# Attention and a conditional convolution on one core: turns of four key tiles, eight probability buffers, streamed experts

## The chip, the cores and the metric

The kernel runs on one core of one Trainium2 chip. The metric is the time of one execution on the device in microseconds (us), the median of the runs shown.

## The reference, cut to what matters

Sixteen images of 256 channels and 32 x 32 pixels (N = 1024 positions) go through two layers, all in float32.

```python
# layer 0: attention, 4 heads of 64
xn = group_norm(x, gn_w, gn_b)                       # 32 groups
q, k, v = split(qkv_w @ xn + qkv_b)
p = softmax(q^T k / 8)                               # 1024 x 1024 per head
x = x + proj_w @ (v p^T) + proj_b
# layer 1: conditional bottleneck, 8 experts
rw = sigmoid(mean(x) @ router_w^T + router_b)        # per image
w1, w2, w3 = sum_e rw[e] * experts[e]                # 1x1, 3x3, 1x1
h = relu(bn1(conv1x1(x, w1))); h = relu(bn2(conv3x3(h, w2)))
out = relu(bn3(conv1x1(h, w3)) + x)
```

## The kernel before

**Stages.** The program is a prologue, one section per image (`sections`: images 0, 1 and 15 written out, 2 to 14 a loop) and an epilogue. A section does the attention of its image i; the projection, the router and the convolutions of image i-1 and the normalisation, Q, K and V of image i+1 are "side jobs" in it. Every engine walks the same tables in the same order, so a table fixes the order of each engine's instructions, and semaphores do the rest.

**Attention.** A section has 4 blocks (2 head pairs x 2 halves of 512 queries) of 8 key tiles, so 32 steps. A step s on TensorE is `scores` (L574 and L577, two float32r matmuls for each of two heads, into one of two S slots; `scores(s)` waits for the exponential of step s-2), then ScalarE's exponential over 1,024 columns (L654) into one of PBUF probability buffers, GpSimd's running sum of the probabilities (L447, `psum_p`), and `pv` (L590, true float32, two heads in the two 64-column halves of the array). `z` (L492) sums `psum_p` over the keys with ones. The scores have the row maximum subtracted inside the matmul: for every step TensorE also fills MS with Q K^T of a later block (`max_fill`, L555, AHEAD = 4 + 8 steps ahead), VectorE takes the maximum (L763), `row` (L503, L767) turns eight of them into a row, and two DMAs of SyncE (L336) carry it into Q2, where the second scores matmul (L577) of the block's first step waits for it. MS is one buffer, so fill n+1 waits for maximum n:

```python
pe.wait_ge(max_read, 32 * i + 8 * b + m)
```

**Turns.** A turn is two steps: scores(2t+2), fill, MID jobs; scores(2t+3), fill, LATE jobs; pv(2t), pv(2t+1); HALVES jobs. The jobs all use one PSUM bank, SB. Each carries `held`, the job before it, and waits on TensorE until that one has been read out of SB:

```python
for k, bi, bf in before:
    pe.wait_ge(read[k], done(k, bi, bf))
```

**Who reads the jobs.** ScalarE reads `qk` (L668 to a raw copy, L672 twice to the float32r part), `v` (L678, L679), `z` (L683), `conv1` (L694, relu into `hpad`) and `conv2` (L698). VectorE reads `proj` (L805; after the fourth also `pool2` L810 and `poolb` L813, which `router` L514 waits for), `router` (L816), `conv3` (L825, then relu L702 and a store L361 into one of 3 y slots), `gna`, `gnb` and `row`. VectorE further does `split_x` (L755), the low parts of Q and K (L800), the gates (L841, L843), the weighted sum of experts (`mix_experts`, L851 and L854, 8 per image), the copies into `mix3` (L859), `stats` (L749) and `normalise_o` (L836). The exact places on VectorE are: maximum, jobs of the half step, then the extras of the tables MIX, RECIPROCAL, NORMALISE, SPLIT, STATS.

**DMA.** SyncE issues everything in the order of the tables: the copies `dup` of Q and K to the other partition half, `rows`, the round trip of z for the reciprocals (`move_z`, `spread_z`: rz to zc, reciprocal L831 on 64 x 16, z_dram, back as rz), `shift_h` (hpad's lower half to the upper one shifted by one, before conv2), the stores and the loads of x, V and, once, all 8 experts (`ex`, 24 KB per partition).

Of the kernel before, what the change touches and what calls it, by code (L numbers as in the profile page):

```python
# [36 lines left out]
P = 128  # L37
# [21 lines left out]
PBUF = 4  # L59
# [10 lines left out]
TURNS = STEPS // 2  # L70
# [10 lines left out]
EPILOGUE = ([("z", 0, 3)] + [("proj", 0, f) for f in range(4)] + [("router", 0, 0), ("conv1", 0, 0),  # L81
# [15 lines left out]
def build(nc, x, vecs, router_b, wqkv, wproj, wrouter, experts, neg_eye, group_avg, out):  # L97
    ctx = ExitStack()
    with ctx:
# [16 lines left out]
        ex = sb("ex", [P, E, MIX])  # L116
# [13 lines left out]
        x_lo = sb("x_lo", [P, CC, N], F32R)  # L130
        Q1 = sb("Q1", [P, HEADS, N], F32R)
# [5 lines left out]
        prob = sb("prob", [P, PBUF, 2, HALF])  # L137

# [48 lines left out]
        xin_loaded = sem("xin_loaded")  # L187
        x2_loaded = sem("x2_loaded")
# [16 lines left out]
        h_saved = sem("h_saved")  # L205
# [62 lines left out]
        def jobs_of(place, t, first, last):  # L268
            return [j for j in place.get(t, []) if not (first and j[1] < 0) and not (last and j[1] > 0)]

        def all_jobs(t, first, last):
            return jobs_of(MID, t, first, last) + jobs_of(LATE, t, first, last) + jobs_of(HALVES, t, first, last)
# [29 lines left out]
        def _(sp):  # L302
# [36 lines left out]
            def shift_h(i):  # L339

                sp.wait_ge(read["conv1"], i + 1)
                sp.dma_start(hpad[64:128, 0:PAD], hpad[0:64, 1:PAD + 1]).then_inc(h_saved, 16)

# [13 lines left out]

            def store(i, f):
                oc, hf = f // NH, f % NH
                sp.wait_ge(y_ready, 4 * i + f + 1)  # L360
                sp.dma_start(out[i, :, oc, px(hf)], y[:, f % YBUF, :]).then_inc(y_stored[f], 16)  # L361

            def section(i, first, last):
                load_v1(i)
                if not last:
                    load_xin(i + 1)
                for t in range(TURNS):
                    for kind, di, f in all_jobs(t, first, last):
# [4 lines left out]
                        if kind == "conv1":  # L373
                            shift_h(i + di)
                        if kind == "conv3":
                            store(i + di, f)
                        if kind == "z":
                            move_z(i + di, f)
                    if t in RECIPROCAL and in_range(RECIPROCAL[t][0], first, last):
                        spread_z(i + RECIPROCAL[t][0], RECIPROCAL[t][1])  # L380
                load_x2(i)
# [9 lines left out]
            sp.dma_start(ex[:, :, :], experts).then_inc(rest_loaded, 16)  # L391
# [5 lines left out]
            move_z(B - 1, BLOCKS - 1)  # L397
            spread_z(B - 1, BLOCKS - 1)
            shift_h(B - 1)
# [55 lines left out]
        def _(pe):  # L455
# [9 lines left out]
            def job(kind, i, f, before, bank=SB[:, :], at_end=False):  # L465
# [38 lines left out]
                elif kind == "bias":  # L504

                    pe.wait_ge(rest_loaded, 16 * 5)
# [14 lines left out]
                elif kind in ("conv2a", "conv2"):  # L521
                    if kind == "conv2a":
                        pe.wait_ge(h_saved, 16 * i + 16)
# [90 lines left out]
            def section(i, first, last):  # L614

                kind, di, f = all_jobs(TURNS - 1, isinstance(i, int) and i == 1, False)[-1]
                held = [("row", 0, 0)] if first else [(kind, i - 1 + di, f)]
                for t in range(TURNS):
                    for half, place in ((0, MID), (1, LATE)):
                        if t < TURNS - 1:  # L620
                            scores(i, 2 * t + 2 + half)
                        elif not last:
                            scores(i + 1, half)
                        at = fill_at(i, 2 * t + half, last)
                        if at:
                            max_fill(*at)
                        for kind, di, f in jobs_of(place, t, first, last):
                            job(kind, i + di, f, held)
                            held = [(kind, i + di, f)]
                    pv(i, 2 * t)  # L630
                    pv(i, 2 * t + 1)
                    for kind, di, f in jobs_of(HALVES, t, first, last):
                        job(kind, i + di, f, [] if kind == "conv2" else held)
                        held = [(kind, i + di, f)]

            sections(pe, section)
            pe.wait_ge(read["z"], BLOCKS * B - 1)
# [6 lines left out]
        def _(act):  # L644
# [16 lines left out]
            def job(kind, i, f, bank=SB[:, :]):  # L661
# [25 lines left out]
                elif kind == "conv1":  # L687
                    act.wait_ge(filled["conv1"], i + 1)
                    rows_hf = H // NH
                    for hf in range(NH):  # L690
                        at = (1 + hf * rows_hf) * PW + 1
                        dst = hpad[0:64, at:at + rows_hf * PW].rearrange("p (r w) -> p r w", w=PW)[:, :, 0:W]
# [30 lines left out]
            def section(i, first, last):  # L723
                for t in range(TURNS):
                    for half, place in ((0, MID), (1, LATE)):
                        if t < TURNS - 1:
                            exps(i, 2 * t + 2 + half)
                        elif not last:
                            exps(i + 1, half)
                        for kind, di, f in jobs_of(place, t, first, last):  # L730
                            job(kind, i + di, f)
                        if t == NORM and not last:
                            normalise(i + 1, half)
                    if t % 4 == 3:
                        save_o(i, t // 4)
                    for kind, di, f in jobs_of(HALVES, t, first, last):
                        job(kind, i + di, f)
# [7 lines left out]
        def _(dve):  # L745
# [82 lines left out]
            def reciprocal(i, f):  # L828

                dve.wait_ge(z_moved[f], 32 * i + 32)  # L830
                nc.vector.reciprocal(zc[:, f % 2, :], zc[:, f % 2, :]).then_inc(rz_ready, 1)  # L831

            def normalise_o(i, f):
                dve.wait_ge(z_back[f], 32 * i + 32)
# [11 lines left out]
            def mix_experts(i, e0, e1):  # L846
                for e in range(e0, e1):
                    if e == 0:
                        gates(i)
                        wait(dve, filled["conv3"], 4 * i)  # L850
                        nc.vector.tensor_scalar(mix[:, :], ex[:, 0, :], rw[:, 0:1], None, ALU.mult).then_inc(mix_chain, 1)  # L851
                    else:
                        dve.wait_ge(mix_chain, E * i + e)
                        nc.vector.scalar_tensor_tensor(out=mix[:, :], in0=ex[:, e, :], scalar=rw[:, e:e + 1], in1=mix[:, :],  # L854
# [7 lines left out]
            def mix_last(i):  # L862

                gates(i)
                n = E * i
                for c0, c1 in ((0, M1), (M1, M1 + M2), (M1 + M2, MIX)):
                    for e in range(E):
                        if e == 0:
                            if c0 == 0:
                                dve.wait_ge(filled["conv3"], 4 * i)  # L870
                            op = nc.vector.tensor_scalar(mix[:, c0:c1], ex[:, 0, c0:c1], rw[:, 0:1], None, ALU.mult)
                        else:
                            dve.wait_ge(mix_chain, n)
                            op = nc.vector.scalar_tensor_tensor(out=mix[:, c0:c1], in0=ex[:, e, c0:c1], scalar=rw[:, e:e + 1],
# [42 lines left out]
            dve.wait_ge(rest_loaded, 16 * 5)  # L917

            def section(i, first, last):
                mixed = 0  # L920
                for t in range(TURNS):
                    for half, place in ((0, MID), (1, LATE)):
                        at = fill_at(i, 2 * t + half, last)
                        if at:
                            max_reduce(*at)
                        for kind, di, f in jobs_of(place, t, first, last):
                            job(kind, i + di, f)
                        if half == 1 and t in RECIPROCAL and in_range(RECIPROCAL[t][0], first, last):
                            reciprocal(i + RECIPROCAL[t][0], RECIPROCAL[t][1])
                        if half == 1 and t in NORMALISE and in_range(NORMALISE[t][0], first, last):  # L930
                            normalise_o(i + NORMALISE[t][0], NORMALISE[t][1])
                        if not last:
                            if half == 1 and t == STATS_0:
                                stats(i + 1, 0)
                            if half == 1 and t == STATS_1:
                                stats(i + 1, 1)
                            if t == SPLIT:
                                split_x(i + 1, half)
# [72 lines left out]
```

## Time and profile before

| | |
|---|---|
| median of 3 runs (lowest to highest) | 2105.53 us (2100.91 to 2111.38) |
| profiled execution, its own time | 2096.82 us |
| its span | 2095.0 us |
| mean granted TensorE clock | 0.984 |
| busy: TensorE, VectorE, GpSimd, ScalarE | 94%, 69%, 53%, 50% |
| chain that ended last | PE 79%, DVE 12%, issue 5%, DMA 2%, ACT 2% |
| HBM | 34 GB/s over the span |

The first `conv1` matmul of an image is at 254.1, 380.5, 506.4, 632.2, 759.6 us and so on to 1900.0: one image takes 125.8 to 127.4 us. The epilogue begins at about 2044. Busy TensorE is an upper bound of its work, since the ends of matmuls are modelled; the distances between starts are what counts. In the rows further down, a timeline row has the start and the duration in us, the number of merged instructions (x8) and in brackets the idle time ahead of it with what ended it.

### The profile page before, as it was taken

Reading aid. Unit: us, or ns where it says so; the run is one execution under the profiler, and the core shown is the slowest. Engines: PE = TensorE matmul, PEld = TensorE weight load, DVE = VectorE, ACT = ScalarE, POOL = GpSimd, SP = SyncE. Lnnn points to the kernel's source line nnn. Section 1 sums busy time; section 2 is a strip of 40 time slices with the busy share of each in tenths; the row PEclk is TensorE's granted clock in tenths of the full one; section 3 lists DMA queues with packets and bytes.
Section 4 is the critical chain, followed back from the end, with each engine's and each line's share of the span. In section 5 each row is a group of like instructions: output and inputs, shape, how many; then the busy total and the mean of one; then the engine's idle time right before and its main releaser. Section 6 shows DMA issues by size and latency. Waiting matters only on the chain.

```text
span 2095.0 us, 26308 instructions
## 1 busy us (share of the span) xinstructions
PE 1960.1 (94%) x8072; PEld 1061.8 (51%) x8072; DVE 1440.0 (69%) x1638; ACT 1045.7 (50%) x1346; POOL 1118.7 (53%) x533
## 2 busy tenths in 40 slices
PE   4999999999999999999999989999899999999994
PEld 3555555545555455555555545455554555545431
DVE  5658768486784957758586785857858587685743
ACT  3555545454555444555454555454554455554441
POOL 3665555464555545555464564645555555554660
PEclk9999999999999999999999999999999999999997
DMA  3112131121313012130121312113130121301201
GB/s 137 42 26 82 36 101 26 44 74 31 101 31 96 20 36 91 32 105 20 41 81 31 101 30 65 47 36 96 31 101 18 38 87 34 101 24 43 56 27 61
DMA packets 65694, 119.35 MB, mean 57 GB/s; under 512 B 20480, under 2 KB 21248, under 8 KB 65536
## 3 DMA queue, kind: packets, MB, share of 16 engines
q1 hardware_dynamic: 65664, 118.97, 19.4%
q8 instruction: 16, 0.26, 0.1%
q14 instruction: 14, 0.11, 0.0%
HBM read 54.68 MB, written 17.04 MB: 34 GB/s over the span
## 4 chain that ended last, share of the span: by engine, by line
PE 79%; DVE 12%; issue 5%; DMA 2%; ACT 2%; DVEq 0%; SPq 0%; POOL 0%; ACTq 0%
PE PV L590 19%; PE SB L461 12%; PE S L574 11%; PE MS L555 10%; PE S L577 9%; PE SB L498 5%; PE SB L532 4%; DVE mx L763 4%; DVE mix L854 3%; PE SB L492 3%; PE SB L540 3%; DVE rden L841 2%; PE SB L519 1%; DVE o L836 1%; DVE x_lo L755 1%
## 5 line engine op out<-in xcount | busy, mean ns | idle before, releaser
L447 POOL TENSOR_TENSOR psum_p<-psum_p,prob 128x1024 f32<-128x1024 f32 x384 | 931.1, 2425 | 596.4 <-ACT prob L654 589.0
L763 DVE TENSOR_REDUCE mx<-MS 128x1 f32<-128x1024 f32 x500 | 609.9, 1220 | 416.1 <-PE MS L555 413.9
L654 ACT ACTIVATE prob<-S 128x1024 f32<-128x1024 f32 x512 | 523.7, 1024 | 405.1 <-PE S L577 398.6
L590 PE MATMUL PV<-prob,V 128*64 128x512 f32 x2048 | 506.9, 617 | 0.0
L574 PE MATMUL S<-Q,K 128*128 128x512 f32 x1024 | 455.1, 444 | 2.5 <-DVE mx L910 2.5
L577 PE MATMUL S<-Q,K 128*128 128x512 f32 x1024 | 406.1, 397 | 0.3 <-DMA Q<-mrow 0.3
L555 PE MATMUL MS<-K,Q 128*128 128x512 f32 x1000 | 327.8, 409 | 73.3 <-DVE mx L763 73.2
L574 PEld LDWEIGHTS S<-Q,K 128*128 128x128 f32 x1024 | 194.3, 190 | 264.9 <-issue 231.4
L447 POOL TENSOR_TENSOR psum_p<-prob 128x1024 f32<-128x1024 f32 x64 | 151.7, 2370 | 311.3 <-ACT prob L654 311.3
L590 PEld LDWEIGHTS PV<-prob,V 128*64 128x64 f32 x2048 | 125.5, 137 | 266.4 <-issue 240.5
L555 PEld LDWEIGHTS MS<-K,Q 128*128 128x128 f32 x1000 | 176.5, 188 | 162.5 <-DVE mx L763 131.2
L577 PEld LDWEIGHTS S<-Q,K 128*128 128x128 f32 x1024 | 195.3, 191 | 35.4 <-issue 7.2
L800 DVE TENSOR_TENSOR K<-qk_raw,K 64x512 fp32r<-64x512 f32 x128 | 108.0, 844 | 75.5 <-ACT K L672 74.4
L800 DVE TENSOR_TENSOR Q<-qk_raw,Q 64x512 fp32r<-64x512 f32 x128 | 123.6, 966 | 47.7 <-ACT Q L672 46.2
L854 DVE SCALAR_TENSOR_TENSOR mix<-ex,rw,mix 128x768 f32<-128x768 f32 x105 | 136.0, 1295 | 1.0
L668 ACT ACTIVATE qk_raw<-SB,vec 128x512 f32<-128x512 f32 x124 | 85.3, 688 | 78.0 <-PE SB L461 77.1
L498 PE MATMUL SB<-o,wp 128*128 128x512 f32 x240 | 112.7, 592 | 0.0
L836 DVE TENSOR_TENSOR o<-o,rz 128x512 f32<-128x512 f32 x64 | 88.4, 1382 | 30.4 <-DMA rz<-z_dram 30.4
L461 PE MATMUL SB<-x_hi,w_hi 128*128 128x512 f32 x248 | 98.7, 398 | 3.7 <-DVE x_lo L755 3.7
L461 PE MATMUL SB<-x_lo,w_hi 128*128 128x512 f32 x248 | 98.1, 395 | 0.0
L461 PE MATMUL SB<-x_hi,w_lo 128*128 128x512 f32 x248 | 98.0, 395 | 0.0
L659 ACT ACTIVATE o<-PV 128x512 f32<-128x512 f32 x64 | 38.0, 593 | 104.8 <-PE PV L590 104.8
(126 smaller groups left out, 1879.8 us busy)
## 6 DMA issues: line engine op xcount, KB each, us to landing
xin<-in_x_dram SPq DMA_DIRECT2D x16, 1024.0 KB, 8.7
K<-K SPq DMA_DIRECT2D x128, 128.0 KB, 2.2
Q<-Q SPq DMA_DIRECT2D x128, 128.0 KB, 2.3
rz<-z_dram SPq DMA_DIRECT2D x128, 128.0 KB, 2.9
x<-in_x_dram SPq DMA_DIRECT2D x16, 1024.0 KB, 6.2
out_dram<-y SPq DMA_DIRECT2D x64, 256.0 KB, 2.1
V<-v_next SPq DMA_DIRECT2D x16, 512.0 KB, 6.5
hpad<-hpad SPq DMA_DIRECT2D x16, 289.0 KB, 3.1
```

The lines of the kernel that those rows point to most:

```text
L447: nc.gpsimd.tensor_tensor(acc, first_in, prob[:, s % PBUF, :, :], ALU.add).then_inc(add_done, 1)
L461: last = nc.tensor.matmul(dst, wl(w, c), xl(m, c), start=(k == 0), stop=(k == 3 * CC - 1))
L498: last = nc.tensor.matmul(bank, wp[:, c, oc * P:oc * P + P], o[:, c, px(hf)], start=(c == 0), stop=(c == CC - 1))
L555: last = nc.tensor.matmul(MS[:, nh, :], Q1[:, h, q0:q0 + P], K1[:, h, px(nh)], start=True, stop=True)
L574: nc.tensor.matmul(S[:, s % 2, a, :], K1[:, h, kt * P:kt * P + P], Q1[:, h, px(hf)], start=True, stop=False)
L577: last = nc.tensor.matmul(S[:, s % 2, a, :], K2[:, h, kt * P:kt * P + P], Q2[:, h, px(hf)], start=False, stop=True)
L590: last = nc.tensor.matmul(PV[own(a), :], V[:, b // NH, kt, a * D:a * D + D], prob[:, s % PBUF, a, :], start=(kt == 0), stop=(kt == KT - 1))
L654: nc.scalar.activation(prob[:, s % PBUF, :, :], S[:, s % 2, :, :], ACT.Exp, scale=D ** -0.5).then_inc(exp_done, 1)
L763: nc.vector.reduce_max(mx[:, b % 2, m:m + 1], MS[:, :, :], AX.XY).then_inc(max_read, 1)
L800: last = nc.vector.tensor_tensor(dst, qk_raw[own(a), f % 2, :], hi[own(a), h, px(hf)].bitcast(F32), ALU.subtract)
L836: nc.vector.tensor_tensor(o[:, f // NH, px(f % NH)], o[:, f // NH, px(f % NH)], rz[:, f % 2, :], ALU.mult).then_inc(o_norm, 1)
L854: nc.vector.scalar_tensor_tensor(out=mix[:, :], in0=ex[:, e, :], scalar=rw[:, e:e + 1], in1=mix[:, :], op0=ALU.mult, op1=ALU.add).then_inc ...
```

## The change

- A turn is four steps (BATCH = 4): four times scores, fill, side jobs; then four pv; then HALVES. The tables MID and LATE become PLACES, by step.
- PBUF goes from 4 to 8 (16 KB more per partition). To make room, `ex` holds 2 experts instead of 8; SyncE loads each expert again for every image (384 KB), after the accumulation of the one two before it. The last image's experts go into buffers that are free by then.
- `z` of a block comes right behind its last four pv; block 3's no longer lies in the next section, and the last one's reciprocal is taken on 128 x 512 in place, without the round trip.
- `conv1` is followed directly by `z` of block 2. The DMA `shift_h` goes; ScalarE writes `hpad` with four instructions instead of two.
- `conv3` comes as two pairs (steps 29 and 30), `proj` 3 at step 9 and `router` at step 10, `row` 1 at step 4, normalisation on ScalarE at 10 and 11, its split on VectorE at 11 and 12, the first `qk` of the next image at 13, the gates at 13, the eight experts at 14, 15, 16, 18, 19, 20, 21, 22.
- In SyncE's queue `move_z` of block 3 moves to the section's head, behind the load of xin, and the load of x2 to behind the last store.

```diff
-PBUF = 4
+PBUF = 8
-MID = {0: [("qk", 0, 5)], 1: [("qk", 0, 7)], 2: [("row", 0, 1)], 3: [("proj", -1, 2)], 4: [("gnb", 1, 0)],
-       5: [("router", -1, 0)], 6: [("row", 0, 2)], 8: [("qk", 1, 0)], 9: [("qk", 1, 2)], 10: [("row", 0, 3)],
-       11: [("v", 1, 1)], 12: [("v", 1, 3)], 13: [("conv3", -1, 0)], 14: [("row", 1, 0)], 15: [("qk", 1, 4)]}
-LATE = {0: [("qk", 0, 6)], 1: [("proj", -1, 0)], 2: [("proj", -1, 1)], 3: [("gna", 1, 0)], 4: [("proj", -1, 3)],
-        8: [("qk", 1, 1)], 9: [("qk", 1, 3)], 10: [("v", 1, 0)], 11: [("v", 1, 2)], 13: [("conv3", -1, 1)],
-        14: [("conv3", -1, 2)], 15: [("conv3", -1, 3)]}
-HALVES = {0: [("z", -1, 3)], 4: [("z", 0, 0)], 8: [("z", 0, 1)], 11: [("conv1", -1, 0)],
-          12: [("conv2a", -1, 0), ("conv2", -1, 0)], 13: [("z", 0, 2)]}
+BATCH = 4
+TURNS = STEPS // BATCH
+PLACES = {0: [("qk", 0, 5)], 1: [("qk", 0, 6)], 2: [("proj", -1, 0)], 3: [("proj", -1, 1)], 4: [("row", 0, 1)], 5: [("gna", 1, 0)],
+          6: [("proj", -1, 2)], 7: [("qk", 0, 7)], 8: [("gnb", 1, 0)], 9: [("proj", -1, 3)], 10: [("router", -1, 0)],
+          12: [("row", 0, 2)], 13: [("qk", 1, 0)], 15: [("qk", 1, 1)], 17: [("qk", 1, 2)], 19: [("qk", 1, 3)],
+          20: [("row", 0, 3)], 21: [("v", 1, 0)], 22: [("v", 1, 1)], 23: [("v", 1, 2)], 24: [("v", 1, 3)],
+          28: [("row", 1, 0)], 29: [("conv3", -1, 0), ("conv3", -1, 1)], 30: [("conv3", -1, 2), ("conv3", -1, 3)], 31: [("qk", 1, 4)]}
+HALVES = {1: [("z", 0, 0)], 3: [("z", 0, 1)], 5: [("conv1", -1, 0), ("z", 0, 2)], 6: [("conv2a", -1, 0), ("conv2", -1, 0)], 7: [("z", 0, 3)]}
...
-RECIPROCAL = {1: (-1, 3), 5: (0, 0), 9: (0, 1), 14: (0, 2)}
-NORMALISE = {2: (-1, 3), 6: (0, 0), 10: (0, 1), 15: (0, 2)}
-STATS_0, STATS_1, NORM, SPLIT, AFFINE_STEP = 1, 2, 6, 7, 10
-MIX_MID = {6: 1}
-MIX_LATE = {5: 1, 6: 1, 7: 1, 8: 1, 9: 1, 10: 2}
+SPLIT = {11: 0, 12: 1}
+GATES = 13
+MIXED = {14: 1, 15: 1, 16: 1, 18: 1, 19: 1, 20: 1, 21: 1, 22: 1}
+RECIPROCAL = {1: (-1, 3), 9: (0, 0), 17: (0, 1), 25: (0, 2)}
+NORMALISE = {3: (-1, 3), 16: (0, 0), 23: (0, 1), 27: (0, 2)}
+STATS = {2: 0, 3: 1}
+NORM = {10: 0, 11: 1}
...
+            def load_expert(i, e):
+                wait(sp, mix_chain, E * i + e - 1)
+                sp.dma_start(ex[:, e % 2, :], experts[:, e, :]).then_inc(ex_loaded[e % 2], 16)
...
+                for n in range(STEPS):
+                    if n + 2 < STEPS:
+                        scores(i, n + 2)
+                    elif not last:
+                        scores(i + 1, n + 2 - STEPS)
+                    at = fill_at(i, n, last)
+                    if at:
+                        max_fill(*at)
+                    for kind, di, f in jobs_of(PLACES, n, first, last):
+                        job(kind, i + di, f, held)
+                        held = [(kind, i + di, f)]
+                    if n % BATCH == BATCH - 1:
+                        for s in range(n + 1 - BATCH, n + 1):
+                            pv(i, s)
+                        for kind, di, f in jobs_of(HALVES, n // BATCH, first, last):
+                            job(kind, i + di, f, [] if kind == "conv2" else held)
                             held = [(kind, i + di, f)]
...
-                    for hf in range(NH):
-                        at = (1 + hf * rows_hf) * PW + 1
+                    for hf, upper in ((0, 0), (1, 0), (0, 1), (1, 1)):
+                        at = (1 + hf * rows_hf) * PW + 1 - upper
...
             def reciprocal(i, f):
+                if isinstance(i, int) and (i, f) == (B - 1, BLOCKS - 1):
+                    dve.wait_ge(read["z"], BLOCKS * B)
+                    nc.vector.reciprocal(rz[:, f % 2, :], rz[:, f % 2, :]).then_inc(rz_ready, 1)
+                    return
```

## Rows read from the trace of the kernel before

**Rows 1.** Part 1 of the page: busy time, share of the span, instructions.

```profile
PE 1960.1 (94%) x8072; PEld 1061.8 (51%) x8072; DVE 1440.0 (69%) x1638; ACT 1045.7 (50%) x1346; POOL 1118.7 (53%) x533
```

**Rows 2.** Waits of the whole span: in total, times, longest.

```profile
PE MS L555 <- DVE mx L763: 73.2, 68, 1.9
```

**Rows 3.** Timeline of PE, 1009 to 1014: start, duration, line, operation.

```profile
1009.41 0.28 PE L461 MATMUL SB<-w_lo,x_hi 128*128 128x256 f32 x1
1009.62 1.94 PE L590 MATMUL PV<-prob,V 128*64 128x512 f32 x8
1011.39 1.89 PE L519 MATMUL SB<-x,mix 128*64 128x512 f32 x8
1013.20 0.50 PE L574 MATMUL S<-Q,K 128*128 128x512 f32 x1
1013.54 0.39 PE L577 MATMUL S<-Q,K 128*128 128x512 f32 x1
1013.77 0.39 PE L574 MATMUL S<-Q,K 128*128 128x512 f32 x1
```

**Rows 4.** Timeline of PE, 1077 to 1080: two fills of MS.

```profile
1077.35 0.63 PE L555 MATMUL MS<-K,Q 128*128 128x512 f32 x2
...
1079.30 0.73 PE L555 MATMUL MS<-K,Q 128*128 128x512 f32 x2
```

**Rows 5.** Timeline of DVE, 1078 to 1086.

```profile
1078.02 1.22 DVE L763 TENSOR_REDUCE mx<-MS 128x1 f32<-128x1024 f32 x1 [0.23 <-PE MS L555]
...
1082.17 0.73 DVE L805 SCALAR_TENSOR_TENSOR x<-SB,pbias,x 128x512 f32<-128x512 f32 x1
...
1082.95 2.12 DVE L810 TENSOR_TENSOR pool<-pool 128x2 f32<-128x2 f32 x1
1085.10 0.48 DVE L813 TENSOR_SCALAR poolb<-ones,pool 128x128 f32<-128x128 f32 x2
```

**Rows 6.** Timeline of DVE, one expert accumulated at 1105.

```profile
1105.62 3.14 DVE L854 SCALAR_TENSOR_TENSOR mix<-ex,rw,mix 128x768 f32<-128x768 f32 x1
```

**Rows 7.** Timeline of POOL in the same stretch.

```profile
1105.50 2.44 POOL L447 TENSOR_TENSOR psum_p<-psum_p,prob 128x1024 f32<-128x1024 f32 x1 [3.16 <-ACT prob L654]
```

**Rows 8.** Timeline of ACT, the padded copy after the first convolution.

```profile
1013.32 1.57 ACT L694 ACTIVATE hpad<-SB,bn_c,bn_s 64x512 f32<-64x512 f32 x2 [1.12 <-PE SB L519]
```

**Rows 9.** Timeline of DVE, last image: the row of maxima.

```profile
2006.06 0.27 DVE L767 CAST mrow<-SB 8x128 fp32r<-8x128 f32 x1
```

**Rows 10.** Timeline of PE, last image: the scores that need it.

```profile
2008.75 0.49 PE L577 MATMUL S<-Q,K 128*128 128x512 f32 x1 [0.30 <-DMA Q<-mrow]
```

**Rows 11.** Groups by line and shape: busy, mean ns.

```profile
L668 ACT ACTIVATE qk_raw<-SB,vec 128x512 f32<-128x512 f32 x124 | 85.3, 688 | 78.0 <-PE SB L461 77.1
L672 ACT ACTIVATE K<-qk_raw 64x512 fp32r<-64x512 f32 x128 | 80.6, 630 | 4.7
...
L841 DVE TENSOR_SCALAR rden<-rexp 128x8 f32<-128x8 f32 x16 | 33.7, 2104 | 0.3 <-ACT rexp L686 0.3
...
L831 DVE RECIPROCAL zc<-zc 64x16 f32<-64x16 f32 x64 | 15.2, 238 | 5.8 <-DMA zc<-rz 5.3
```

**Rows 12.** DMA issues, 200 to 2000: KB each, us to landing.

```profile
V<-v_next SPq DMA_DIRECT2D x14, 512.0 KB, 6.5
```

**Rows 13.** Chain of waits near the end: start, us, what.

```profile
2044.98 0.61 ACT rz L683
...
2056.96 0.70 DVE o L836
...
2074.80 3.02 DMA hpad<-hpad
```

**Rows 14.** Timeline of PE, 974 to 978: a wait for DVE and what follows.

```profile
974.70 0.73 PE L555 MATMUL MS<-K,Q 128*128 128x512 f32 x2 [1.73 <-DVE mx L763]
975.37 3.10 PE L590 MATMUL PV<-prob,V 128*64 128x512 f32 x8
```

**Rows 15.** Busy time by stretch: last columns granted clock, DMA share, GB/s.

```profile
976.00:980.00 4.00, 4.00 (x13) 1.58 (x8) 4.00 (x4) 0.60 (x1) 0.47 (x1) 0.57 0.00 0
```

More of the change, by code:

```diff
@@ L268, in jobs_of @@
         def jobs_of(place, t, first, last):
-            return [j for j in place.get(t, []) if not (first and j[1] < 0) and not (last and j[1] > 0)]
-        def all_jobs(t, first, last):
-            return jobs_of(MID, t, first, last) + jobs_of(LATE, t, first, last) + jobs_of(HALVES, t, first, last)
+            return [j for j in place.get(t, []) if in_range(j[1], first, last)]
         def in_range(di, first, last):
@@ L363, in section @@
             def section(i, first, last):
-                load_v1(i)
                 if not last:
                     load_xin(i + 1)
-                for t in range(TURNS):
-                    for kind, di, f in all_jobs(t, first, last):
+                if not first:
+                    move_z(i - 1, BLOCKS - 1)
+                load_v1(i)
+                mixed = 0
+                for n in range(STEPS):
+                    for kind, di, f in jobs_of(PLACES, n, first, last):
                         if kind == "qk":
@@ L390, in _ @@
             sp.dma_start(rbias[:, :], router_b).then_inc(rest_loaded, 16)
-            sp.dma_start(ex[:, :, :], experts).then_inc(rest_loaded, 16)
+            for e in range(2):
+                sp.dma_start(ex[:, e, :], experts[:, e, :]).then_inc(ex_loaded[e], 16)
             for f in range(5):
@@ L614, in section @@
             def section(i, first, last):
[L616 to L628, printed above, removed]
-                            held = [(kind, i + di, f)]
[L630 to L634, printed above, removed]
+                held = [("row", 0, 0)] if first else [("z", i - 1, BLOCKS - 1)]
+                for n in range(STEPS):
+                    if n + 2 < STEPS:
[5 more added lines that the diff above has]
+                        max_fill(*at)
+                    for kind, di, f in jobs_of(PLACES, n, first, last):
+                        job(kind, i + di, f, held)
+                        held = [(kind, i + di, f)]
+                    if n % BATCH == BATCH - 1:
+                        for s in range(n + 1 - BATCH, n + 1):
+                            pv(i, s)
+                        for kind, di, f in jobs_of(HALVES, n // BATCH, first, last):
+                            job(kind, i + di, f, [] if kind == "conv2" else held)
+                            held = [(kind, i + di, f)]
             sections(pe, section)
-            pe.wait_ge(read["z"], BLOCKS * B - 1)
+            pe.wait_ge(read["z"], BLOCKS * B)
             pe.wait_ge(o_saved, BLOCKS * B)
@@ L723, in section @@
             def section(i, first, last):
[L724 to L730, printed above, removed]
-                            job(kind, i + di, f)
[L732 to L737, printed above, removed]
+                for n in range(STEPS):
+                    if n + 2 < STEPS:
+                        exps(i, n + 2)
+                    elif not last:
+                        exps(i + 1, n + 2 - STEPS)
+                    for kind, di, f in jobs_of(PLACES, n, first, last):
+                        job(kind, i + di, f)
+                    if n in NORM and not last:
+                        normalise(i + 1, NORM[n])
+                    if n % KT == KT - 1:
+                        save_o(i, n // KT)
+                    if n % BATCH == BATCH - 1:
+                        for kind, di, f in jobs_of(HALVES, n // BATCH, first, last):
+                            job(kind, i + di, f)
             sections(act, section)
@@ L916, in _ @@
             dve.wait_ge(consts_set, CONSTS_SET)
-            dve.wait_ge(rest_loaded, 16 * 5)
+            dve.wait_ge(rest_loaded, 16 * 4)
             def section(i, first, last):
                 mixed = 0
[L921 to L938, printed above, removed]
-                        count = (MIX_LATE if half else MIX_MID).get(t, 0)
-                        if count and not first:
-                            mix_experts(i - 1, mixed, mixed + count)
-                            mixed += count
```

100 lines of the change are left out of this document (72 added, 28 removed).

## The prediction, blind

> **What bounds the kernel now.** I read the page first: TensorE is busy 94% of the span, VectorE 69% [rows 1], so TensorE's own instruction stream sets the time and every wait in it counts in full. The waits of the whole span come next: the only one that TensorE repeats is the fill of MS behind VectorE's maximum, 73.2 us in 68 waits [rows 2], some 4.9 us for each of the 15 images after the first. Everything else is hidden or lies in prologue and epilogue. Then the timelines of PE and DVE, for three things: what it costs TensorE to go from float32r matmuls to the float32 ones and back [rows 3]; how soon one fill of MS can follow another [rows 4, 5]; and what a VectorE instruction costs while GpSimd adds [rows 6, 7]. The chain of waits serves for the end alone [rows 13].
>
> Two rules come out of the rows. **Fill to fill**: the fill at 1077.35 has its maximum from 1078.02 to 1079.24, the next fill starts at 1079.30 [rows 4, 5]. So fills are at least 1.95 us apart, and a step without a job is only 0.46 + 0.93 = 1.39 us of TensorE (two MS matmuls and four score matmuls at 0.23 [rows 3]): it waits 0.56. What stands in VectorE's queue between two maxima adds to that once it exceeds TensorE's own work. Before, pv followed every second fill, so every second gap was 1.8 us longer; after, three gaps in four have no pv. **VectorE beside GpSimd**: the accumulation of one expert took 3.14 us from 1105.62, with a GpSimd addition of 2.44 us from 1105.50 [rows 6, 7]; the part after that addition is only 0.8. Tiny operations do the same: 2.12 us for pool2 [rows 5], 2.10 us mean for the gates' first [rows 11].
>
> **The change, part by part, per middle image (14 of them), in us.**
>
> *Turns.* TensorE enters float32 at 0.21 after the last 256-column float32r matmul, where half of 0.23 would do, leaves conv1 0.04 later than pv (1.81 against 1.77), and the first score matmul then takes 0.34 instead of 0.23 [rows 3]: 0.24, with the start of the group about 0.3 for each group of float32 work. Turns of four save 8 of 16 such groups. But LATE jobs lay directly ahead of pv and shared its group; single float32 jobs inside turns go from 8 (four rows, proj 2, gnb, router, conv3 0) to 12 (steps 2, 4, 5, 6, 8, 9, 10, 12, 20, 28, 29, 30). Net four groups less: **-1.2**.
>
> *conv1, then z.* Both use SB, and z waits until ScalarE has read conv1. Two hpad writes took 1.57 [rows 8]; four take 3.14, and nothing stands on TensorE between the two jobs. Before, scores, a fill and 1.5 us covered it. **+3.1**. Queued behind z are the scores of step 26; their exponential comes later by the same.
>
> *conv3 in pairs.* The second one waits for VectorE's read of the first, and VectorE takes the maximum first. With F the start of the fill: maximum done F + 1.89, read 0.73 (the row of the same form [rows 5]), so the second starts at F + 2.65; it could at F + 1.41 (0.55 for the fill, 0.86 for a conv3, as the two pairs of half-array matmuls). 1.25, twice: **+2.5**.
>
> *Router at step 10.* proj 3 ends at F + 2.36, VectorE reads it until F + 3.2, pool2 2.12, poolb 0.48 [rows 5]: F + 5.8. TensorE wants the router at F + 3.95. Before, pv, z and a step lay between. With pool2 undisturbed (0.2) it costs nothing; behind a late maximum 2.6. The nearest row is contended: **+1.8**.
>
> *Row at step 4.* A row cast from 2006.06 to 2006.33 let its score matmul start at 2008.75, and TensorE waited [rows 9, 10]: 2.42 through two DMAs. Cast done at F + 2.1, so F + 4.5; wanted at F + 3.05, since only row, gna (0.3 each, an estimate) and one step lie between, no pv. **+1.5** (1.2 to 1.8).
>
> *First qk at step 13.* At step 12 VectorE has the maximum, the row and the second split; the split is a two-input operation of 1.2 (an estimate) to 3.1, the contended one of [rows 6]. It ends at F + 3.4 to 5.3, qk is wanted at F + 2.4. Before it stood four steps before its user's turn and was nearly hidden. **+1.5** (1.0 to 2.9).
>
> *Waits for the maximum.* Lone steps 14, 16, 18, 25, 26: 5 x 0.56 = 2.8. Fill 15: VectorE first needs ScalarE's raw copy 0.69 and high part 0.63, two low parts, the gates 2.1 and 0.2 [rows 11]; maximum 14 ends about 6.3 after qk's end, fill 15 is wanted at 2.3, so 4.0, or 2.1 with the gates undisturbed; I take 3.2, 2.6 beyond the lone step. Steps 16 to 19, with an expert (1.0 to 3.1) and the low parts between maxima: 2.1 more. Steps 0 to 3, with the low parts of qk 5 and 6, two proj reads and statistics: 1.3 (estimate). Together 8.8 less the 4.9 of before: **+3.9** (0 to 9).
>
> *Streamed experts.* 512 KB landed in 6.5 [rows 12]; 384 KB by that 4.9. A load has the time of two experts, some two steps of 2.5 and more, so it is just hidden; without that cover up to 1 per expert. SyncE waits for `mix_chain` ahead of later copies of Q and K, which have ten steps. **0** (to +2). Eight buffers: GpSimd needs 2.4 per step [rows 7] against a mean step of 3.9, so it never held the exponentials long; **0**.
>
> *Clock.* A wait of 1.73 was followed by pv of 3.10 instead of 1.94, at a mean granted clock of 0.57 of full speed, so mostly at the 1.2 GHz level [rows 3, 14, 15]. There TensorE would have waited for VectorE anyway; behind conv1 it would not. **+0.5** (0 to 3). The Trainium skill, page "TensorE: Matmul & The Clock Gate", section "HAM oscillation — how this bites in real kernels", says that a loop whose matmul bursts are separated by waits falls back to the slow clock in every pass. If that held here for each of the new waits, rival C below is what it would give.
>
> Sum: -1.2 + 3.1 + 2.5 + 1.8 + 1.5 + 1.5 + 3.9 + 0.5 = 13.6, times 14 = 190.
>
> *Ends.* Image 0 has no jobs of an image before it, hence more lone steps (11 instead of 4): +4. The last image has no fills from step 20 on, but conv1, router and row remain: +7. Epilogue: from the end of z's copy, 2045.59, to VectorE's multiplication at 2056.96, 11.4 us of DMA round trip go [rows 13]; in comes a reciprocal of 512 columns. 64 x 16 took 0.238 [rows 11]; bounds 0.70 (one plain pass [rows 13]) and 32 times 0.238 = 7.6; I take 2.5, nearer to the pass, because a fixed part must lie in the 0.238. -8.9. hpad: 3.02 of DMA for 1.57 of ScalarE [rows 8, 13]: -1.4. Ends together +1. The Trainium skill, page "VectorE: DVE Perf Modes", section "First, the fixed hardware budget", says that a reciprocal is an iterative division with a repeat count of 8; an estimate from the page, 512 x 8 cycles at 0.96 GHz, is 4.3 us. By it the gain is 7.1 and the sum 2 us more.
>
> Against the profiled execution's 2096.8: 2096.8 + 190 + 1 = 2288. The median of the runs shown is 8.7 above it, so **2296**. A difference under 0.5% (10 us) I count as none.
>
> **Rivals.**
> - **A, the forecast** (0.60): 2296.
> - **B, only the fixed waits** (0.15): VectorE's contended operations fall clear of GpSimd and its queue keeps up; what stays is conv1, conv3, the row and -1.2: 5.9 x 14 = 83, 2189. For it: VectorE is idle 31% of the span. Against: nearly every tiny operation in rows 5 and 11 shows the 2 us.
> - **C, the clock falls in most turns** (0.13): three such stretches an image at 1.2 to 1.5 each, 4 more per image: 2352. For it: rows 14 and 15 need a wait of 1.73 only. Against: where TensorE waits for VectorE anyway, the slow stretch is absorbed.
> - **D, faster** (0.07): the place is MS. Each new wait of TensorE for SB is time in which VectorE works off its queue, so the waits for the maximum, 4.9 per image, go to none, and router, row and split find their data ready: -1.2 + 3.1 + 2.5 - 4.9 = -0.5 per image, 7 in all, and 10 of the epilogue: 2088. It decides if the waits of MS after are under some 20 us in total. Against: the lone steps alone give 2.8 per image.
> - **E, no difference** (0.05): the change does not do what it says; the pv of four steps do not run as one group and the new waits replace old ones of the same length: 2105.
>
> **The numbers.** A, B and C are slower: 0.88; E is the same; D faster. The range takes B's value less 29 for milder bounds at its bottom, and at its top A with the upper bounds of router, split, maximum and clock (13.6 + 0.8 + 1.4 + 2.5 + 2.5 = 20.8 per image, 2397): 2160 to 2400. It leaves D and E out, 0.12, and the tails.
>
> **What would show it.** Right: 128 pv groups instead of 256; TensorE waits of some 3 us for hpad once per image; SB waits in both conv3 pairs; a wait for poolb and one for the row's DMA in most images; waits for the maximum near 130 us; a period near 140 instead of 126; TensorE's busy share under 90%. Wrong: a period under 128, no wait for hpad, or waits for the maximum not above 73 us.

## The result, and the profile after

The changed kernel takes 2460.75 us (2458.82 to 2462.09, 4 runs) against 2108.24 us (2100.91 to 2111.38, 4 runs): ratio 1.1677, 95% interval 1.1643 to 1.1712. Slower was forecast, 2296 with a range of 2160 to 2400; the loss is nearly twice the forecast one. The profiled execution of the kernel after spans 2458.6 us, that of the kernel before 2095.0. From parts 1 and 4 of the page of the kernel after:

```profile
PE 2037.5 (83%) x8072; PEld 1114.5 (45%) x8072; DVE 1573.3 (64%) x1638; ACT 1073.9 (44%) x1378; POOL 1141.6 (46%) x533
...
PE 61%; DVE 18%; issue 12%; ACT 5%; DMA 2%; SPq 1%; DVEq 0%; ACTq 0%; POOL 0%
```

TensorE was busy 94% [rows 1]; now 83%, and VectorE holds 18% of the chain that ended last, against 12%. Waits of the whole span after (who waited, for whom: us in total, times, longest). Before, only the first of them was of any size in the loop [rows 2]; the fourth came to 3.7 us in 7 waits:

```profile
PE MS L589 <- DVE mx L796: 158.1, 159, 4.9
PE SB L548 <- DVE poolb L846: 68.4, 15, 4.7
PE SB L526 <- ACT hpad L727: 49.6, 15, 3.3
PE SB L495 <- DVE x_lo L788: 35.7, 15, 2.6
PE SB L574 <- DVE y L858: 33.8, 31, 1.1
PE S L611 <- DMA Q<-mrow: 29.7, 34, 1.6
```

Every wait that the prediction named is there. Where the 363.6 us between the two spans are: start to the first conv1, 289.3 against 254.1, +35.2; 13 periods (from one conv1 to the next) of 150.2 against 126.6, +306.9; from the 14th conv1 to the 15th, 141.5 against 115.9, +25.6; the rest -4.1. The second reading is the clock. The 13 periods of the kernel after in one row; first the stretch and its length, last the granted clock (as a share of full speed), the DMA share and GB/s:

```profile
289.30:2242.20 1952.90, 1640.27 (x6556) 898.83 (x6554) 1285.68 (x1313) 869.89 (x1118) 915.44 (x416) 0.95 0.22 67
```

Before it was 0.99. Over the whole span the mean is 0.947 against 0.984. TensorE stands at one of two levels, 2.4 GHz or half of it, so a stretch's time at 1.2 GHz is (1 - clock) x 2 x its length. For the 13 periods (0.9546 after, 0.9927 before) that gives 13.7 us per image after and 1.8 before. The periods of the kernel before show both cases: those of 125.9 us hold a stretch at 1.2 GHz ([rows 15] lie in one) and 4.0 us of waits, those of 127.4 hold none and 6.4 us of waits. There the slow stretch cost nothing in sum: its periods are the shorter ones.

**One wait in detail**: the router, which needs `poolb`, the row that VectorE makes of the pooled image (`pool2`). Timelines of PE, DVE and POOL of the kernel after:

```profile
1274.04 0.63 PE L589 MATMUL MS<-K,Q 128*128 128x512 f32 x2
...
1279.30 1.02 PE L548 MATMUL SB<-wr,poolb 128*128 128x8 f32 x4 [4.64 <-DVE poolb L846]
```

```profile
1270.87 1.76 DVE L825 TENSOR_TENSOR gvar<-gvar_of,gvar_in 128x2 f32<-128x2 f32 x1
...
1274.47 2.10 DVE L843 TENSOR_TENSOR pool<-pool 128x2 f32<-128x2 f32 x1
1276.61 2.64 DVE L846 TENSOR_SCALAR poolb<-ones,pool 128x128 f32<-128x128 f32 x2
```

```profile
1274.21 4.76 POOL L481 TENSOR_TENSOR psum_p<-psum_p,prob 128x1024 f32<-128x1024 f32 x2
```

GpSimd had two additions in a row. pool2 waited out the first, as it did before [rows 5], and poolb, which took 0.48 before, the second: 2.64. `gvar` of the normalisation, just ahead of step 9's maximum, took 1.76 and held that maximum until 1272.56; in the kernel before it took 1.77 at the same place. After such a wait the clock is down. Stretches of the kernel after, granted clock third from the right:

```profile
1274.00:1279.00 5.00, 0.66 (x3) 0.20 (x2) 4.93 (x5) 1.02 (x1) 4.85 (x3) 0.94 0.00 0
1279.00:1283.00 4.00, 3.70 (x10) 2.67 (x10) 1.55 (x5) 2.42 (x3) 0.00 (x0) 0.50 0.08 26
```

TensorE worked from 1279.30 at 1.2 GHz, on matmuls that nothing else was going to hold up.

### The profile page after: what moved, and what is told of

The parts are those of the page before. It is cut to its first block, busy times and chain, and to the rows that moved or that the text cites. A ratio compares the mean times of both kernels' runs of the same rounds, so it can differ in the third digit from the quotient of the medians.

```text
span 2458.6 us, 26643 instructions
## 1 busy us (share of the span) xinstructions
PE 2037.5 (83%) x8072; PEld 1114.5 (45%) x8072; DVE 1573.3 (64%) x1638; ACT 1073.9 (44%) x1378; POOL 1141.6 (46%) x533
## 4 chain that ended last, share of the span: by engine, by line
PE 61%; DVE 18%; issue 12%; ACT 5%; DMA 2%; SPq 1%; DVEq 0%; ACTq 0%; POOL 0%
PE PV L624 19%; PE SB L495 8%; PE MS L589 8%; PE S L608 7%; DVE mx L796 7%; PE S L611 6%; PE SB L566 3%; PE SB L526 3%; PE SB L532 2%; DVE Q L833 2%; DVE x_lo L788 2%; ACT hpad L727 2%; PE SB L574 1%; DVE mix L894 1%; ACT qk_raw L701 1%
## 5 line engine op out<-in xcount | busy, mean ns | idle before, releaser
L481 POOL TENSOR_TENSOR psum_p<-psum_p,prob 128x1024 f32<-128x1024 f32 x384 | 953.3, 2483 | 970.7 <-ACT prob L687 956.4
L624 PE MATMUL PV<-prob,V 128*64 128x512 f32 x2048 | 487.3, 620 | 0.0
L589 PE MATMUL MS<-K,Q 128*128 128x512 f32 x1000 | 355.8, 438 | 158.1 <-DVE mx L796 158.1
L608 PE MATMUL S<-Q,K 128*128 128x512 f32 x1024 | 482.3, 471 | 2.4 <-DVE mx L953 2.4
L611 PE MATMUL S<-Q,K 128*128 128x512 f32 x1024 | 430.4, 420 | 29.7 <-DMA Q<-mrow 29.7
L608 PEld LDWEIGHTS S<-Q,K 128*128 128x128 f32 x1024 | 206.2, 201 | 177.5 <-issue 142.2
L624 PEld LDWEIGHTS PV<-prob,V 128*64 128x64 f32 x2048 | 140.7, 142 | 288.5 <-issue 278.9
L611 PEld LDWEIGHTS S<-Q,K 128*128 128x128 f32 x1024 | 207.6, 203 | 90.5 <-DMA Q<-mrow 40.9
L894 DVE SCALAR_TENSOR_TENSOR mix<-ex,rw,mix 128x768 f32<-128x768 f32 x105 | 174.8, 1665 | 4.5 <-DMA ex<-in_experts_dram 3.4
L833 DVE TENSOR_TENSOR K<-qk_raw,K 64x512 fp32r<-64x512 f32 x128 | 97.7, 763 | 94.5 <-ACT K L705 93.6
L876 DVE TENSOR_TENSOR o<-o,rz 128x512 f32<-128x512 f32 x64 | 100.5, 1570 | 35.5 <-DMA rz<-z_dram 34.9
L526 PE MATMUL SB<-psum_p,ones 128*64 128x512 f32 x256 | 74.6, 665 | 49.6 <-ACT hpad L727 49.6
```

Of the source, the lines that this page charges most:

```text
L481: nc.gpsimd.tensor_tensor(acc, first_in, prob[:, s % PBUF, :, :], ALU.add).then_inc(add_done, 1)
L526: last = nc.tensor.matmul(bank[own(a), :], ones[:, 0:D], psum_p[:, f % 2, a, :], start=True, stop=True)
L589: last = nc.tensor.matmul(MS[:, nh, :], Q1[:, h, q0:q0 + P], K1[:, h, px(nh)], start=True, stop=True)
L608: nc.tensor.matmul(S[:, s % 2, a, :], K1[:, h, kt * P:kt * P + P], Q1[:, h, px(hf)], start=True, stop=False)
L611: last = nc.tensor.matmul(S[:, s % 2, a, :], K2[:, h, kt * P:kt * P + P], Q2[:, h, px(hf)], start=False, stop=True)
L624: last = nc.tensor.matmul(PV[own(a), :], V[:, b // NH, kt, a * D:a * D + D], prob[:, s % PBUF, a, :], start=(kt == 0), stop=(kt == KT - 1))
```

## The experiments

All columns behind the ratio are in us per image, over the 13 periods from the first conv1 to the 14th of the profiled execution: "period" is the distance between two conv1, "waits" TensorE's idle time in it, "low" the time at 1.2 GHz by the formula above. Each ratio is to executions of the kernel before that ran beside that kernel.

| kernel | median us | ratio to before (95%) | period | waits | low |
|---|---|---|---|---|---|
| before | 2108.24 | 1 | 126.6 | 5.1 | 1.8 |
| after | 2460.75 | 1.168 (1.164 to 1.171) | 150.2 | 24.0 | 13.7 |
| e1 z first | 2449.96 | 1.164 (1.159 to 1.168) | 150.2 | 21.9 | 20.2 |
| e2 proj 3 early | 2501.27 | see below | 152.5 | 24.9 | 18.4 |
| e3 turns of two | 2280.06 | 1.083 (1.078 to 1.088) | 139.3 | 14.4 | 8.4 |
| e4 filled waits | 2404.15 | 1.142 (1.137 to 1.146) | 146.7 | 16.2 | 1.6 |
| e5 two, conv apart | 2194.65 | 1.043 (1.038 to 1.047) | 133.7 | 11.3 | 3.4 |
| e6 before, streamed | 2107.96 | 1.001 (0.999 to 1.003) | 126.6 | 5.0 | 2.4 |
| e8 before, lighter | 2047.90 | 0.973 (0.969 to 0.977) | 123.8 | 3.7 | 0 |
| e9 before, pv by four | 2217.05 | 1.050 (1.046 to 1.053) | 133.7 | 12.6 | 1.3 |
| e10 lighter still | 2058.12 | 0.975 (0.972 to 0.977) | 124.5 | 4.1 | 0 |
| e11 short sums | 2245.18 | 1.063 (1.060 to 1.066) | 136.6 | 14.2 | 6.0 |

**e3, turns of two.** Only the length of a turn in the changed kernel:

```diff
-BATCH = 4
-HALVES = {1: z0, 3: z1, 5: conv1 + z2, 6: conv2, 7: z3}
+BATCH = 2
+HALVES = {3: z0, 7: z1, 11: conv1 + z2, 13: conv2, 15: z3}
```

> The changed kernel with BATCH = 2: everything else (tables by step, eight buffers, streamed experts, conv1 and z together, conv3 in pairs) stays. Theory (turns of four starve the loop of fill and maximum of the cover that pv gave every second step): waits for the maximum fall from 10 to about 5 us per image, poolb from 4.5 to 2.7, the row's DMA from 1.8 to about 0.2, less half clock 2, and eight more float32 groups cost 2.4: 10.8 - 2.4 = 8 us per image: 2340 (2310 to 2370). hpad and conv3 waits stay. Rival (the places of the side jobs did the harm, not the turns): under 2 us per image better, 2430 to 2480.

The kernel gained 181 us, 10.9 per image: more than the theory's 8. Its waits:

```profile
PE MS L589 <- DVE mx L796: 112.5, 102, 3.1
...
PE SB L548 <- DVE poolb L846: 6.5, 14, 0.5
```

The row's wait went as said, poolb's fell further (to 0.5, not 2.7), hpad and conv3 stayed. At the same place as above, two additions of GpSimd now stand 0.9 us apart (1177.00 and 1180.28), and poolb takes 0.48 again. The maxima fell by 2.6 us per image (9.9 to 7.3), not by 5: in the section of image 6, 6.2 us of them lie in steps 15 to 19, where VectorE has the low parts of K and Q and the experts. The time at 1.2 GHz fell by 5.3. So, with the tables of the change, the turn's length is worth half of the loss (181 of 352 us), and what the other edits cost in turns of two is the other half.

**e9, the mirror.** The kernel before with the pv of four steps together, on top of e6:

```diff
-                    pv(i, 2 * t)
-                    pv(i, 2 * t + 1)
+                    if t % 2 == 1:
+                        for s in range(2 * t - 2, 2 * t + 2):
+                            pv(i, s)
```

> The kernel before with eight buffers and streamed experts (e6, 2108 us), its own tables, and only the pv of four steps together at every second turn's end: the batching alone, the mirror of e3. Theory (pv every second step is the cover of fill and maximum; bunched it is lost in 8 gaps of an image, against 8 float32 groups of 0.3 us saved, of which LATE jobs keep some): waits for the maximum from 4.8 to 10 or more, the row's DMA 1 us, slow clock 2 more: +6 us per image, 2200 (2160 to 2240). Rival (turns of four are good, the tables of the change spoil them): 2060 to 2105.

The time is as the theory said (+109 us on e6, 7.1 per image; by the ratios to the kernels before that ran beside them, some 100), the mechanism is not:

```profile
PE S L611 <- DMA Q<-mrow: 70.3, 48, 2.3
PE MS L589 <- DVE mx L798: 54.0, 76, 4.0
PE SB L526 <- ACT qk_raw L703: 37.8, 30, 1.3
```

From e6 to e9 the waits for the maximum fell (4.4 to 3.3 per image), while the row's DMA rose from 0.4 to 4.4, and z, now right behind a LATE job on the same bank, waits for its reader (3.9). What pv covered in these tables was above all these. That TensorE's new waits let VectorE catch up on the maxima, as rival D had it, fits, but it gave back 1.1 us for 8.7 of new waits. The time at 1.2 GHz did not rise (2.4 to 1.3). Bunched pv thus cost 109 us with the tables of before and 181 with those of the change: its share of the loss depends on where the jobs stand.

**e5, the convolution's jobs apart**, in turns of two:

```diff
-11: conv1 + z2, 13: conv2        29: conv3 0 + conv3 1, 30: conv3 2 + conv3 3, 31: qk 4
+11: conv1, 12: conv2, 13: z2     26: conv3 0, 27: conv3 1, 29: conv3 2, 30: qk 4, 31: conv3 3
```

> The changed kernel with turns of two as in e3, and conv1 (after step 23), conv2 (25) and z of block 2 (27) in turns of their own, conv3 as four single jobs (26, 27, 29, 31), qk 4 at 30, z of block 2 inverted at 29 and applied at 31. Theory: the waits for hpad (3.3 us per image) and for conv3's readers (2.3) go, and with them about 1.5 of slow clock: 7 us per image, 2175 (2155 to 2200), against 2280 for e3. Rival (the maxima take over what the bank waits gave VectorE): at least half of it comes back as waits for the maximum, 2225 or more.

The gain was 5.6 per image of the 7. hpad still holds `v` for 1.7, since one step does not cover four hpad writes, and z waits 0.7 for VectorE's read of conv3. This kernel is still some 90 us slower than before; which of the edits left in it costs that, no run separates.

**e1, z ahead of conv1** in the changed kernel, with turns of four.

```diff
-5: [("conv1", -1, 0), ("z", 0, 2)]
+5: [("z", 0, 2), ("conv1", -1, 0)]
```

> The changed kernel with z of block 2 ahead of conv1 instead of behind it (2461 us before this edit). Theory (each new wait of TensorE for the shared bank counts in full, and its slow-clock stretch too): the 3.32 us wait for hpad goes, some 0.7 us of waiting for z's copy comes, and the half-clock stretch behind it goes (z took 1.62 instead of 1.03, the next scores 0.8 more): 3.3 - 0.7 + 1.3 = 3.9 us per image, 15 images: 2402 (2395 to 2415). Rival (VectorE's queue is the real limit and TensorE's bank waits are its slack): waits for the maximum take the place of the hpad wait, under 15 us in all, 2446 or more.

The time lies in the rival's range, but neither mechanism came. The hpad wait falls only to 1.65 (v of step 24 inherits it), z's copy costs 0.7, the waits for the maximum fall from 9.9 to 8.7 instead of rising. The waits are 2.1 less, and the period is the same 150.2. The clock took it back: the time at 1.2 GHz rose from 13.7 to 20.2 per image. Of it TensorE was working 12.3 in the one and 16.2 in the other, and as the same work takes twice as long there, half of the 3.9 more, 2.0, is lost: what was won. The 11 us come from the last image and the epilogue.

**e2, proj 3 at step 7, qk 7 at step 9.**

```diff
-7: [("qk", 0, 7)], ... 9: [("proj", -1, 3)]
+7: [("proj", -1, 3)], ... 9: [("qk", 0, 7)]
```

> The changed kernel with proj 3 at step 7 and qk 7 at step 9, so that four pv and z lie between proj 3 and the router again. Theory: the 4.55 us wait for poolb goes nearly whole, with the slow stretch behind it (pv of that turn took 4.73 instead of 3.65): 4.5 + 1.5 = 6 us per image, 2371 (2355 to 2395). Rival: the chain behind the router (gates' inputs, normalisation, split) is what matters and only moves, so that the waits for the split and the maximum grow by half of it: 2415 or more.

The wait for poolb is gone, but those for the maximum rise from 158.1 in total to 242.2, not by half of it but by more than all. The time is the rival's; its mechanism is so in part only, since the split's wait stays at 2.4. What grew is one wait at step 11, 5.3 us in every image. It is the same contention with another victim: the low parts of Q, VectorE's share of qk 7, now come at step 9 and wait out the two additions, and maximum 10 stands behind them. In the kernel after they took 1.48 from 1264.89, with an addition that ended at 1265.13.

```profile
1151.31 5.53 DVE L833 TENSOR_TENSOR Q<-qk_raw,Q 64x512 fp32r<-64x512 f32 x2 [0.57 <-ACT Q L705]
```

```profile
1151.17 5.12 POOL L481 TENSOR_TENSOR psum_p<-psum_p,prob 128x1024 f32<-128x1024 f32 x2
```

The time stands on two levels: periods of 153.6 in the first images and 150.2 later in one trace, and executions from 2461.0 to 2507.9, so no ratio is given. The clock tells the two levels apart. One period of each, columns as above:

```profile
912.60:1066.20 153.60, 128.46 (x508) 69.99 (x506) 97.49 (x102) 66.91 (x86) 71.28 (x32) 0.93 0.22 65
1679.50:1829.70 150.20, 125.47 (x508) 68.22 (x506) 97.47 (x102) 66.92 (x86) 70.95 (x32) 0.95 0.22 67
```

The waits are nearly the same (25.1 and 24.7); the time at 1.2 GHz is 20.5 and 13.7. TensorE was working 16.8 and 10.2 of it, and half of the difference, 3.3, is nearly the whole 3.4 between the periods.

**e4, filled waits.** 40 matmuls per image into a bank that nobody reads then, placed inside the three longest waits:

```diff
+            def keep_busy(i, blocks, count):
+                wait(pe, o_saved, BLOCKS * i + blocks)
+                for k in range(count):
+                    nc.tensor.matmul(PV[:, :], w_hi[:, 0, 0:P], w_hi[:, 1, 0:HALF], start=True, stop=True)
```

> The changed kernel with idle TensorE time filled: 16 float32r matmuls into the PV bank ahead of the router, 12 between conv1 and z, 12 ahead of the fill of step 18, in images 1 to 15; nobody reads them. They take 9.2 us per image at full clock, all of it within the measured waits of 4.6, 3.3 and 3.6 us. Theory A (the lower granted clock costs some 5 us per image): granted clock rises from 0.947 to 0.98 and the time falls by 2 to 5 us per image, 2385 to 2430. Rival (the half-clock stretches lie where TensorE waits anyway): the time does not fall, 2455 to 2480.

Middle of e4, columns as above:

```profile
287.20:2194.60 1907.40, 1697.41 (x7076) 961.10 (x7074) 1279.91 (x1313) 869.28 (x1118) 914.88 (x416) 0.99 0.23 68
```

There are 520 more matmuls in the records, and the kernel takes 57 us less. The fillers are 9.2 us per image (40 at 0.23); waits and fillers together are 25.4 against 24.0, and all else fell from 126.2 to 121.4. So 4.8 us per image of the loss were work done at 1.2 GHz. That fits the clock: of the 13.7 us at that level in the kernel after TensorE was working 12.3, here 1.4, and half of the difference is 5.4. The time at that level fell to that of before. Theory A holds, at about 5 us.

**e11, short sums.** GpSimd adds 8 of 512 columns per head; the softmax sums of the others are left out.

```diff
-nc.gpsimd.tensor_tensor(acc, first_in, prob[:, s % PBUF, :, :], ALU.add)
+nc.gpsimd.tensor_tensor(acc[:, :, 0:8], first_in[:, :, 0:8], prob[:, s % PBUF, :, 0:8], ALU.add)
```

> The changed kernel with GpSimd adding 8 of 512 columns per head instead of all (the softmax sums are left out but for these columns), so that its additions are short and keep nobody off: the price of contention in the change. Theory (VectorE's two-input and tiny operations wait out GpSimd's additions, and TensorE waits for them): the wait for poolb falls from 4.65 to under 1 us, for the split from 2.4 to 1, for the maximum from 10 to 5, with less slow clock: 12 us per image, 2280 (2240 to 2340). Rival (the order of the queue alone makes the waits): under 3 us per image, 2415 or more. hpad, conv3 and row waits stay in both.

```profile
PE MS L589 <- DVE mx L796: 97.5, 115, 2.5
```

Per image the wait for poolb is 0.2, for the split 0.7, for the maxima 6.2 (after: 4.7, 2.4, 9.9); hpad, conv3 and the row stay. In all it is 216 us less, clock included. So 10 of the 24 us of waits come from VectorE's contention with GpSimd. How much of the change's 352 us it makes up is not shown: the kernel before has such contention too, and no run took GpSimd's additions out of it. Its waits could have given 5.1 per image at most, all its idle time.

**e6, eight buffers and streamed experts alone** in the kernel before: `PBUF = 8`, `ex` for two experts, `load_expert` as in the change.

> The kernel before with only eight probability buffers and the experts streamed two at a time; tables, turns and sums unchanged. Theory (streaming is hidden, buffers never held anybody): the same within 0.5%, 2095 to 2115, no wait of VectorE for expert loads over 1 us per image. Rival (46 MB more of DMA in SyncE's one queue delay the copies of Q and K, the rows and the z round trip): 2 us per image or more, 2135 or more.

There is no difference that can be measured. The expert loads land in 3.3 us.

**e8, a version faster than both.** The kernel before with

```diff
-NORMALISE = {2: (-1, 3), 6: (0, 0), 10: (0, 1), 15: (0, 2)}
-MIX_MID = {6: 1}
+NORMALISE = {2: (-1, 3), 11: (0, 0), 12: (0, 1), 15: (0, 2)}
+MIX_MID = {11: 1}
```

and, in the epilogue, the reciprocal in place and four hpad writes, as in the change.

> The kernel before with three edits that the readings suggest: one expert goes from step 12 to 22, the multiplications by 1/z of blocks 0 and 1 go to steps 23 and 25 where VectorE idles, and the epilogue takes the last reciprocal in place and writes hpad with four ScalarE instructions. Theory (VectorE's work between two maxima is what TensorE waits for): waits for the maximum fall from 4.9 to 2.5 us per image, the end by 8 us: 2063 (2045 to 2080), faster than before. Rival (the waits only move, or the slow clock fills them up): the end's 8 us alone, 2090 to 2105.

It is 2.7% faster than before, 56 to 60 us where 45 were forecast: the waits for the maximum are down from 4.8 to 3.2 per image, the middle has no stretch at 1.2 GHz any more (1.8 us before), and the end went from 53.6 to 46.4 us between the last two conv1. **e10** moved one more expert and both multiplications later:

```diff
-MIX_LATE = {5: 1, 6: 1, 7: 1, 8: 1, 9: 1, 10: 2};  NORMALISE 11: (0, 0), 12: (0, 1)
+MIX_LATE = {5: 1, 6: 1, 7: 1, 8: 1, 10: 2, 11: 1}; NORMALISE 12: (0, 0), 14: (0, 1)
```

> e8 (2048 us) with one more expert moved, from step 19 to 23, and the multiplications of blocks 0 and 1 to steps 25 and 29. Theory: the 1.45 us wait for the maximum of step 20 goes in 14 images, conv1 may wait up to 0.5 for the experts: 2034 (2025 to 2048). Rival (conv1 waits for the late experts as long as the maximum did): 2045 to 2060.

This is the rival: a wait of conv1 for the experts, 1.4 per image, took the place of 0.9 of the maximum. The kernel is no faster than e8; the two ratios' intervals overlap.

## Why the prediction was wrong

Three steps failed in size: the clock's "+0.5", the router's "+1.8", and the ends' "+1". Per middle image, after less before:

| term | forecast | measured |
|---|---|---|
| conv1, then z | 3.1 | 3.3 |
| conv3 in pairs | 2.5 | 2.2 |
| row | 1.5 | 1.6 |
| first qk | 1.5 | 2.2 |
| router | 1.8 | 4.7 |
| waits for the maximum | 3.9 | 5.1 |
| turns and clock together | -0.7 | 4.6 |
| sum | 13.6 | 23.6 |

- *What held.* The list of waits: each of the six is there, three within 0.3. Streaming and buffers cost 0, as said (e6).
- *Waits for the maximum.* The sum of 8.8 against 9.9 is luck in part. The rule "a lone step waits 0.56" gave 2.8 of it, for steps 14, 16, 18, 25 and 26; in the section of image 6, steps 14, 16 and 25 wait for nothing, 26 for 0.4 and 18 for 3.6. The other large one, fill 15, was put at 3.2 and took 2.5.
- *Router* (the step "pool2 2.12, poolb 0.48 [rows 5]: F + 5.8"). That poolb would meet an addition too was left out: it took 2.64, 2.2 more. `gvar` ahead of step 9's maximum was left out as well and made the rest later by 0.4; in the kernel before it stood there too (1.77), hidden. F + 8.4 was measured and TensorE was ready at F + 3.8: the 4.64 of the row above. That turns of four put GpSimd's additions back to back there, and that this is the cause, is borne out by e3 (poolb 0.48, wait 0.5) and e11 (4.7 down to 0.2).
- *Clock* (the step "+0.5"), the largest miss. Rows 14 and 15 showed a wait of 1.73 followed by the low level, and I charged that as covered. In the kernel before it is covered; in the change the work behind most of the waits is TensorE's own. e4 prices it at 4.8, and the time at 1.2 GHz rose from 1.8 to 13.7. Rival C had the mechanism with a chance of 0.13 and nearly the size (4 on top of the 0.5); together with the forecast's waits it belonged into the main case. By itself it would not have saved the number: C's 2352 is still 109 short. The Trainium skill, page "TensorE: Matmul & The Clock Gate", section "HAM oscillation — how this bites in real kernels", says that a loop whose matmul bursts are separated by waits falls back to the slow clock in every pass. The trace agrees: behind the router's wait the granted clock is 0.50 in the stretch at 1279, and each of the 13 periods has 13.7 us at 1.2 GHz.
- *Turns* (-1.2). Without clock losses and waits, the rest of a period is 121.4 in e4 and 121.5 before. A group of 16 pv took 3.49 to the next start, two of 8 took 3.54 (twice the 1.77 of [rows 3]), or 0.4 in eight groups. The gain was between 0.1 and 0.4 and so at most a third of what I gave it credit for.
- *Ends* (+1), measured +31. The section after image 0's starts at 180.7 instead of 162.0, +18.6 against +4; the 14 middle sections take 332.4 more (23.7 each); from the start of the last section on (2285.6 instead of 1934.6) it is 12.5 more, where the sum had 3 less. At the front, up to these starts, TensorE waits 13.9 us for the maximum and 3.1 for the row's DMA, where before it waited 2.5 for the maximum; I had priced each lone step at 0.56. In the last image conv1 comes 16.7 later within its section instead of 7. Only the epilogue's round trip was as said: from the end of z's copy (2420.23) to VectorE's multiplication (2423.64) it is 3.4 us instead of 11.4. The reciprocal of 512 columns took 3.36 where I took 2.5:

```profile
2420.26 3.36 DVE rz L865
```

  The estimate from the Trainium skill, page "VectorE: DVE Perf Modes", section "First, the fixed hardware budget", was 4.3, from its repeat count of 8; the measured 3.36 lies under it.
- *Rivals.* B and E fell: VectorE's queue did not keep up, and the time is 17% longer. D fell as well: the waits for the maximum did not go. The exchange of waits on which D rests is there in parts, in e9 (1.1 back for 8.7) and the other way round in e2. The range missed because I took router and clock as independent small terms, while both grow with the same packing of the turns: in e3 the router's wait falls from 4.7 to 0.5 and the time at 1.2 GHz from 13.7 to 8.4.

Left open: why a loop settles on one amount of time at 1.2 GHz per image or another (after and e1; the two levels within e2); that this amount makes the periods what they are, the traces show. Also how the last image's 16.7 divide.

## What to carry to other kernels

Where one engine's stream is the bound, bunching its large blocks saves its switches and takes away the cover of every short round trip between them: ask for each wait which block of work lay in it before. Keep loops between two engines (fill and maximum) interleaved with long work, and move the second engine's extras to where it idles: two lines of tables and a shorter epilogue were worth 2.7% here, a rewrite cost 17%. Where VectorE shares the time with GpSimd's additions, moving a job can hand the wait to its neighbour (e2). Price a new wait of TensorE with the slow clock behind it unless something else was late anyway.

## What the runs showed of the hardware

- Matmuls that compute nothing made the kernel 57 us faster; the granted clock in the middle was 0.99 with them and 0.95 without (e4).
- Kernels with waits that differ by 2 us per image had the same period to 0.1 us, the rest being time at 1.2 GHz (after and e1: 13.7 and 20.2 us). One kernel ran with two periods, 153.6 and 150.2, with nearly the same waits: 20.5 and 13.7 us at 1.2 GHz (e2).
- A granted clock of half came after single waits of 1.73 us on a TensorE that was otherwise busy ([rows 14, 15]).
- A reciprocal on 128 x 512 took 3.36 us on VectorE, five plain passes (0.70).
- Operations of two to eight columns on VectorE took 1.76 to 2.22 us beside GpSimd's additions, and 0.16 to 0.20 where GpSimd was idle or its additions short; two of 128 columns together took 2.64 and 0.48. The low parts of Q took 5.53 beside two additions of 5.12 together, and 1.48 with the end of one.
